# Two graph layers on one core: projection in one piece, gates ahead of the copy, fewer warm-ups, one store moved to ScalarE

## The reference, cut to what matters

```
h, g = x @ W_loop.T, (x @ W_loop.T) @ Wg_loop.T
vals = (h + b_loop) * sigmoid(g + bg_loop)
x    = layernorm(x + relu(adj.T @ vals))            # layer 0
x    = layernorm(x + (adj @ x) @ weight[0] + bias)  # layer 1
```

## Time and profile before

| what | us |
|---|---|
| median of 3 runs | 158.95 |
| lowest and highest of them | 158.8, 159.37 |
| the profiled execution's own time | 159.41 |
| its span | 157.7 |

### The profile page before, as it was taken

One profiled execution on the slowest core, in us unless ns is written; L12 is line 12 of the kernel. 1 busy time (PEld: TensorE's weight loads), 2 busy tenths in 40 slices (PEclk: granted clock), 3 DMA queues, 4 the chain that ended last, 5 costly groups with the idle time before them and its releaser, 6 DMA issues.

```text
span 157.7 us, 3520 instructions
## 1 busy us (share of the span) xinstructions
PE 148.8 (94%) x1040; PEld 136.7 (87%) x1040; DVE 124.1 (79%) x325; ACT 122.8 (78%) x255; POOL 125.7 (80%) x195
## 2 busy tenths in 40 slices
PE   7999999999999999999999999999999999999910
PEld 3688999999999999999999999999999999999800
DVE  1359988888988888887988888887888878989980
ACT  3357876979797997979797997979797997769850
POOL 0606698797979799797979799797979799797970
PEclk9999999999999999999999999999999999999995
DMA  4899999989797988979797989989693929211053
GB/s 126 292 405 394 370 389 404 390 265 389 198 382 230 331 303 258 354 241 398 177 392 209 356 290 286 340 237 373 192 393 130 381 92 303 86 69 69 4 201 138
DMA packets 19606, 42.73 MB, mean 271 GB/s; under 512 B 2177, under 2 KB 3073, under 8 KB 19585
## 3 DMA queue, kind: packets, MB, share of 16 engines
q1 hardware_dynamic: 14544, 25.76, 48.6%
q0 software_dynamic: 4752, 16.52, 30.3%
q10 hardware_dynamic: 288, 0.20, 0.4%
HBM read 34.08 MB, written 8.39 MB: 269 GB/s over the span
## 4 chain that ended last, share of the span: by engine, by line
POOL 65%; PE 15%; issue 13%; DVE 1%; POOLq 1%; ACT 0%; DVEq 0%
POOL rstd L339 31%; POOL x L353 26%; PE hg_ps L423 7%; POOL adj_sb L326 4%; POOL adjt_sb L333 3%; PE loop_ps L439 2%; PE msg_ps L458 2%; PE msg_ps L413 1%; PE y_ps L497 1%; PE hg_ps L407 1%; POOL rstd L363 1%; POOLq L59 1%; DVE s_sb L808 0%; ACT gate L607 0%; POOLq L234 0%
## 5 line engine op out<-in xcount | busy, mean ns | idle before, releaser
L339 POOL TENSOR_TENSOR rstd<-var,power 128x8 f32<-128x8 f32 (+1 forms) x36 | 53.8, 1496 | 18.5 <-DVE var L787 18.4
L423 PE MATMUL hg_ps<-w_all,xt_sb 128*128 128x256 f32 x256 | 65.7, 382 | 0.0
L353 POOL TENSOR_SCALAR x<-s_sb,mean_neg,rstd 128x128 f32<-128x128 f32 x120 | 52.2, 448 | 3.4
L423 PEld LDWEIGHTS hg_ps<-w_all,xt_sb 128*128 128x128 f32 x256 | 44.6, 193 | 4.1 <-issue 0.3
L626 ACT ACTIVATE out_sb<-z_sb,rstd 128x128 f32<-128x128 f32 x120 | 38.1, 390 | 0.4 <-POOL rstd L339 0.4
L800 DVE TENSOR_TENSOR vals<-hg_ps,gate 128x512 f32<-128x512 f32 x32 | 22.1, 690 | 19.3 <-ACT gate L607 19.3
L439 PEld LDWEIGHTS loop_ps<-vals,adj_sb 128*128 128x128 f32 x256 | 33.3, 191 | 1.9 <-issue 0.2
L598 ACT ACTIVATE hg_ps<-gate_b 128x1024 f32<-128x1024 f32 (+1 forms) x32 | 31.8, 998 | 3.2 <-DVE vals L800 2.6
L458 PEld LDWEIGHTS msg_ps<-adjt_sb,x 128*128 128x128 f32 x248 | 31.4, 191 | 3.1 <-issue 1.5
L439 PE MATMUL loop_ps<-vals,adj_sb 128*128 128x128 f32 x256 | 33.8, 275 | 0.1
L458 PE MATMUL msg_ps<-adjt_sb,x 128*128 128x128 f32 x248 | 33.2, 277 | 0.0
(11 more groups left out here) (64 smaller groups left out, 48.2 us busy)
## 6 DMA issues: line engine op xcount, KB each, us to landing
xt_sb<-x_t_dram SPq DMA_DIRECT2D x32, 256.0 KB, 4.9
x_sb<-x_dram SPq DMA_DIRECT2D x32, 256.0 KB, 4.2
out<-out_sb SPq DMA_DIRECT2D x31, 256.0 KB, 4.7
adj_sb<-adj_dram POOLq DMA_DIRECT2D x15, 512.0 KB, 5.2
adjt_sb<-adj_t_dram POOLq DMA_DIRECT2D x15, 512.0 KB, 6.5
adjt_sb<-adj_t_dram POOLq DMA_DIRECT2D x2, 256.0 KB, 6.7
first_edges<-adj_dram SPq DMA_DIRECT2D x1, 256.0 KB, 4.2
adj_sb<-adj_dram POOLq DMA_DIRECT2D x1, 256.0 KB, 6.3
```

Source lines behind the costliest of these rows:

```text
L339: nc.gpsimd.tensor_tensor(rstd[:, c % RSTD_RING, first:end, :].rearrange("p l b -> p (l b)"), var[:, c % 2, first:end, :].rearrange("p l b ...
L353: done = nc.gpsimd.tensor_scalar(x1[:, q % X1_RING, batch(b)], s_sb[:, q % S_RING, batch(b)], mean_neg[:, c % 2, b:b + 1], rstd[:, c % RST ...
L423: last = nc.tensor.matmul(hg_ps[:, q % 2, b, :], xt_sb[:, q % XT_RING, batch(b)], w_gate, start=False, stop=True, skip_group_check=True)
```

## The change

Four things change.

1. In iterations 4 to 29 PE projects all four graphs of group t in one piece, then runs the messages, the loop sum and the message weights. Before, the messages stood between the two halves of the projection. Iterations 0 to 3 keep their order.
2. ACT runs the gates of group t ahead of the copy of messages of t - 3 in those iterations.
3. Three warm-up matmuls instead of five ahead of the projection of group 0.
4. Group 30's output is written by ACT (norm2, four instructions) and stored from ACT's own DMA queue; DVE's instruction for it and SP's store of it are gone.

```diff
@@ SP
-            sp.wait_ge(out_dve, 1)
-            store(LAST - 1)
             for p in range(2):
                 span = slice(2 * p * P, 2 * (p + 1) * P)
-                sp.wait_ge(out_dve, p + 2)
+                sp.wait_ge(out_dve, p + 1)
@@ PE
-            for _ in range(5):
+            for _ in range(3):
                 nc.tensor.matmul(msg_ps[:, :], warm[:, :], warm_wide, start=True, stop=True)
@@ PE, for t in range(GROUPS - 2), after project(t, (0, 1))
-                else:
-                    messages(t - MSG_LAG)
                 project(t, (2, 3))
-                if t == MSG_LAG:
-                    messages(0)
+                messages(t - MSG_LAG)
                 loop_sum(t - LOOP_LAG)
                 message_weights(t - Y_LAG)
@@ ACT, the same loop
+                gates(t)
                 copy_messages(t - MSG_LAG)
-                gates(t)
@@ ACT, after norm2(GROUPS - 3, every)
+            norm2(GROUPS - 2, every)
+            act.wait_ge(out_done, GROUPS - 1)
+            act.dma_start(out[GROUPS - 2], out_sb[:, (GROUPS - 2) % OUT_RING, :])\
+                .then_inc(out_st[(GROUPS - 2) % OUT_RING], 16)
@@ DVE, at the end
-            last_norm2(LAST - 1, 0, GB, root_count(GROUPS + 2, 1))
```

## The result

| | before | changed |
|---|---|---|
| median of 4 runs each, us | 158.88 | 161.67 |
| lowest to highest | 158.5 to 159.37 | 161.54 to 161.84 |
| changed / before | | 1.0157, 95% interval 1.0127 to 1.0187 |
| profiled execution, us (span) | 159.41 (157.73) | 161.84 (160.09) |

The account below looks back on a forecast made before the run. The prediction took PE, busy without a break in iterations 4 to 29, as the bound. Its terms, +2.85 for the loop, -0.13 for the start and -0.70 for the end, gave +2.02: 158.95 to 161.0 us, range 159.6 to 162.8.

Parts of the forecast that it names:

- The loop's term: Iterations 4 to 29: 26 x 4.53 - 114.93 = +2.85 us.
- The wait on the copy: PE's message weights wait for ACT's copy, 1.02 us against a loop sum of 0.89: 0.12 us in every iteration.
- The hand-over: From the end of ACT's copy to PE's message weights: 0.11 us, taken from iteration 3; the least certain size.
- a short hand-over: Rival in the loop: hand-over 0.06 and wait about 0.08 us or less, total within 0.5%; chance 0.10.
- no wait: Rival in the loop: iteration 3's wait belongs to the start alone, 4.41 us per iteration, 157.85 us in all; chance 0.06.
- ACT falls behind: Rival in the loop: iterations with look delay the copy by 0.3 us in 13 pairs, +3.9, 164.9 us; chance 0.03.
- Two warm-ups fewer: At the start: the first projection comes sooner, worth 0.10 to 0.43 us at the lower clock; taken as -0.13 us.
- near POOL's row: At the start: the first projection load comes near 5.2, as POOL, released by the same transfer, moves at 5.22.
- The late clock: Rival at the start: the clock rises only after projections of groups 0 and 1, 2.8 us more, 163.9 us; chance 0.05.
- Group 30 by ACT: At the end: SP's queue sets the last store; without group 30's store it is issued sooner, -0.70 us.
- all that follows (154.73 to 157.7) comes behind that issue: At the end: everything after SP's last store issue moves with it, so the whole 0.70 us is gained.
- a bonus: At the end: the last root ends some 0.2 us earlier with DVE's multiplication halved, gaining 0.9 instead of 0.70.

Follow-up runs that it names:

- Experiment 3: The changed kernel with the copy of messages cut in two halves, messages of graphs 2 and 3 in another PSUM bank; 158.41 us, ratio 0.9939 to the kernel before.
- experiment 4: The kernel before, projection still in two halves, with only the gates moved ahead of the copy on ACT; 175.19 us in one run.
- experiment 1: The kernel before with only the reorder of PE and ACT, warm-ups and end as before; 162.14 us, ratio 1.0168.
- experiment 2: The changed kernel with the gates put back behind the copy on ACT; 161.32 us, ratio 1.0138 to the kernel before.
- experiment 6: The kernel before with three warm-up matmuls instead of five, nothing else; 159.34 us, ratio 0.9987.
- experiment 9: The changed kernel with the copy in two halves and group 31's second half stored from ACT; 158.29 us, ratio 0.9905 to the kernel before.
- experiment 7: The kernel before with only the change's end, group 30 written and stored by ACT; 158.89 us, ratio 0.9963.
- experiment 10: The changed kernel with the copy in two halves, run once more as a base; 158.28 us, ratio 0.9949 to the kernel before.
- experiment 12: The changed kernel with split copy, group 29 also stored by ACT, group 31's second half multiplied by GpSimd; 158.13 us, ratio 0.9917 to the kernel before.

## Why the prediction was right, point by point

161.67 us stands against a forecast of 161.0. The loop's term came as forecast (+2.79 for +2.85), the two small ones did not (0.00 for -0.13, -0.43 for -0.70), and the other 0.4 is the spread of the executions told above.

**The wait on the copy: right, in mechanism and size.** 0.31 + 0.60 + 0.11 = 1.02 against 0.89; 4.53 us per iteration, +2.79 in all. Experiment 3 takes the wait away by taking away what makes it, and the loss goes; experiment 4 makes it 0.61 by the same arithmetic; experiment 1 shows that no other part is needed. The hand-over was the open size, and iteration 3 was the right row for it: 0.11 to 0.12, not the 0.06 of the earlier trace rows. With that fell the rivals of a short hand-over and of no wait.

**ACT falls behind: no.** Every copy waits for PE, and putting the gates back (experiment 2) leaves the period as it is.

**Two warm-ups fewer: not to be seen.** In the changed kernel's execution the projection began at 6.17, not near 5.2. It needs x transposed and also the biases, of which DVE copies a part into PSUM for group 0, and both came late in that execution. DVE's copy and the row of POOL that the prediction went by:

```profile
5.29 0.69 DVE L750 COPY hg_ps<-gate_b 128x512 f32<-128x512 f32 x1 [1.03 <-DMA gate_b<-gate_bias_dram]
6.01 0.93 POOL L365 DMA_DIRECT2D adj_sb<-adj_dram  x1 [5.45 <-DMA xt_sb<-x_t_dram]
```

POOL's row stands at 6.01 instead of 5.22, and the projection's first load came 0.19 behind the end of DVE's copy. It still reached the loop sum at 9.64, as before, because its passes went at the upper level of the clock from the start on: 16 of them in 3.69 us, against 4.05 before. The step that failed is "near POOL's row": it took one execution's moment for a fixed one, and left DVE's copy out. In the eight traces with three warm-ups POOL's row lies at 5.0 to 6.1; in six of them the projection came 0.18 to 0.19 behind DVE's copy, and in experiments 2 and 6 0.22 behind the landing of x transposed. In experiment 6, the warm-ups alone, it came at 5.44, no sooner than before.

**The late clock: not here, but it exists.** The profiled execution of experiment 9 shows it. PE's matmuls ahead of the first loop sum, in the changed kernel and there:

```profile
6.20 3.69 PE L421 MATMUL hg_ps<-w_all,xt_sb 128*128 128x256 f32 x16 [1.00 <-DVE hg_ps L750]
```

```profile
6.25 5.33 PE L426 MATMUL hg_ps<-w_all,xt_sb 128*128 128x256 f32 x16 [1.05 <-DVE hg_ps L770]
```

Both paused for 1.0 us after three warm-ups; the passes of the second went at 0.43 us each up to about 9.6, and its loop sum came at 11.33. That execution took 160.12 us, where five more of the same kernel took 157.81 to 158.58 and one, without a trace, 160.87. So a pause alone does not decide, and what does is open.

**Group 30 by ACT: the sign right, the size and the reason wrong.** SP's queue did set the last store, issued 0.73 us behind DVE's last output before and still 0.62 behind it after, where 0.05 was foretold. The step that failed is that "all that follows (154.73 to 157.7) comes behind that issue". There were two chains, whose drains lay 0.12 us apart, and the chain of waits on the page pointed at the other one: it ends with POOL's root and DVE's multiplication. Before, DVE's drain at 157.5 was the later one:

```profile
L64 SPq DRAIN  x1: 7/7/7, 157.3 to 157.3; - x1
L64 DVEq DRAIN  x1: 57/57/57, 157.5 to 157.5; - x1
```

After the change both had come 0.42 to 0.44 nearer to P30, for different reasons. SP's second half was issued 0.38 sooner (20.68 against 21.06 after P30), not 0.70, because of the stretched issue ahead of it. DVE's came sooner because the second of the last two roots did, which the earlier trace rows are to be compared with:

```profile
153.76 0.70 POOL L361 TENSOR_TENSOR rstd<-var,power 128x2 f32<-128x2 f32 x1
154.80 0.81 POOL L361 TENSOR_TENSOR rstd<-var,power 128x2 f32<-128x2 f32 x1 [0.34 <-DVE var L869]
155.65 0.43 DVE L877 TENSOR_TENSOR out_sb<-z_sb,rstd 128x256 f32<-128x256 f32 x1 [0.59 <-POOL rstd L361]
```

0.81 instead of 1.08, with 0.43 us of multiplication from just ahead of it on instead of 1.03, which puts DVE's last output 0.26 sooner; the other 0.17 lie between DVE's last branch and its drain, 3.36 before and 3.19 after.

The rule of the Trainium skill (SBUF — State Buffer, Who interferes with whom) that the prediction weighed, by which a VectorE instruction with two SBUF inputs and a GpSimd one that reads SBUF lock each other out, agrees in direction with 1.08 to 0.81. The rows show less than a full lock: the multiplication and the root lie side by side for 0.26 us (154.80 to 155.06), and the root took 0.11 over the 0.70 of one without it. I had set this beside the sum as a bonus; it was the larger part of what DVE's chain gained, and without it the end would have gained at most the other 0.17. No run changed it alone. ACT's own store took 0.37 us to issue and 2.6 to land, and landed ahead of group 31's second half.

## What to carry to other kernels

Count what stands between a producer and the consumer of its copy in the engine's own order: start of the copy, copy and hand-over against the work in between, to a tenth of a microsecond, since a tight loop pays the difference in every iteration. If a reorder opens such a wait, cutting the copy in two can close it again (ratio 0.994 instead of 1.016). At the end of a program look at the closing drain of every engine, not only at the last store: an engine that could stop earlier may be the one that the end waits for.

## What was not expected of the hardware

- DVE's drain came 2.9 to 3.5 us after its last branch (the one that skips the general path) in all 14 traces, whether SP's came 1.1 us ahead of it or 1.0 behind, and an instruction transfer of 0.3 to 0.6 us on queue 14 started 1.8 to 1.9 us ahead of each. The Trainium skill (Runtime: NRT & Kernel Launch, Instruction fetch mechanics) says that a taken branch whose target isn't in the instruction window forces a transfer ahead of going on; the rows agree in order of time, and no run here took the branch away.
- An issue on SP's queue that follows closely on another is stretched from 0.43 to some 1.15 us beside an instruction transfer (experiment 7); one that stands alone isn't. Why is open. It put the last store 0.5 to 0.9 us behind DVE's last output in the changed kernel and experiments 2, 3, 7 and 10, and cost at most 0.13 us of the time there, as DVE's closing was nearly as late or later.
- Of the kernels run, those of experiments 9 and 12 have the lowest ratios (0.9905 and 0.9917); both keep the reorder, three warm-ups and the split copy. Their intervals overlap with each other and with that of the split copy alone (0.9939), so that none of the three is shown to be the fastest.
